# Broadcasting the rows of m by transposes of a repeated column, and denominators in four jobs, in a fused kernel of seven-product matmuls and masked pooling

## The reference, cut to what matters

```
h = gelu(x @ fc1_w.T + fc1_b)                    # 512 -> 2048, exact gelu
x = x + concat(h @ fc2_w.T + fc2_b, h @ experts_w[idx].T + experts_b[idx])   # 384 + 128 columns
attn_in = tanh(x @ W1 + b1)                      # 512 -> 128
scores = attn_in @ v                             # (4, 1024)
mask[j, l] = l <= j | l >= j | l != j            # by the type of the batch
p = softmax(where(mask, scores[l], -1e30), over l)
x = x + (p @ x) / cnt                            # cnt = number of l seen by j
```

## Time and profile before

| | |
|---|---|
| median of the timed runs | 815.1 us |
| profiled execution | 805.86 us |
| its span | 804.2 us |
| mean granted TensorE clock | 0.991 |
| TensorE busy | 781.1 us, 97% |
| VectorE busy | 398.9 us, 50% |
| ScalarE busy | 379.9 us, 47% |
| GpSimd busy | 115.4 us, 14% |
| moved by DMA | 177.11 MB, 220 GB/s |

### The profile page before, as it was taken

The page is one execution under the profiler, slowest core; times in us unless marked ns, Lnnn a source line. Parts: engine busy times, 40 slices in busy tenths (PEclk is TensorE's granted clock), DMA queues, the critical chain, the costliest instruction groups (busy, mean ns, idle before and its releaser), DMA issues.

```text
span 804.2 us, 12318 instructions
## 1 busy us (share of the span) xinstructions
PE 781.1 (97%) x3550; PEld 637.9 (79%) x3550; DVE 398.9 (50%) x681; ACT 379.9 (47%) x641; POOL 115.4 (14%) x157
## 2 busy tenths in 40 slices
PE   6899999999999999999999999999999999999987
PEld 5688887888888888887888888888788888888876
DVE  6855666563453332853535233376245423246665
ACT  6755665443545333552545523445254543344542
POOL 3472230300000130400000022050000002104000
PEclk9999999999999999999999999999999999999998
DMA  7599898777854568866776457886687446697722
GB/s 256 180 365 320 312 348 279 227 229 223 244 173 144 171 197 281 255 208 202 248 215 191 147 162 228 288 246 185 182 277 223 132 150 202 224 282 220 222 67 105
DMA packets 130732, 177.11 MB, mean 220 GB/s; under 512 B 10065, under 2 KB 97633, under 8 KB 130657
## 3 DMA queue, kind: packets, MB, share of 16 engines
q1 hardware_dynamic: 130496, 176.20, 69.5%
q0 software_dynamic: 160, 0.01, 0.1%
HBM read 136.33 MB, written 39.85 MB: 219 GB/s over the span
## 4 chain that ended last, share of the span: by engine, by line
PE 91%; DVE 4%; ACT 2%; issue 1%; DMA 1%; DVEq 0%; SPq 0%; ACTq 0%
PE y L711 14%; PE y L713 14%; PE y L712 14%; PE hA L711 7%; PE hA L713 7%; PE hA L712 7%; PE hF L711 5%; PE hF L713 5%; PE hF L712 5%; PE j L804 2%; DVE xcl L1171 1%; PE j L830 1%; PE j L824 1%; PE j L831 1%; PE j L812 1%
## 5 line engine op out<-in xcount | busy, mean ns | idle before, releaser
L711 PE MATMUL y<-hs,w2c 128*128 128x512 f32 x512 | 202.4, 395 | 3.7 <-DVE w2c L1171 1.4
L713 PE MATMUL y<-hs,w2c 128*128 128x512 f32 x512 | 199.7, 390 | 0.0
L712 PE MATMUL y<-hs,w2c 128*128 128x512 f32 x512 | 199.6, 390 | 0.0
L711 PEld LDWEIGHTS y<-hs,w2c 128*128 128x128 f32 x512 | 96.3, 188 | 26.8 <-DVE hs L1171 4.9
L713 PEld LDWEIGHTS y<-hs,w2c 128*128 128x128 f32 x512 | 96.2, 188 | 20.6
L712 PEld LDWEIGHTS y<-hs,w2c 128*128 128x128 f32 x512 | 96.3, 188 | 19.3
L711 PE MATMUL hA<-xch,w1c 128*128 128x512 f32 x252 | 100.1, 397 | 9.7 <-DVE w1c L1171 5.9
L713 PE MATMUL hA<-xch,w1c 128*128 128x512 f32 x252 | 98.6, 391 | 0.0
L712 PE MATMUL hA<-xcl,w1c 128*128 128x512 f32 x252 | 98.6, 391 | 0.0
L701 POOL TENSOR_TENSOR x1T<-x1T,xnl 128x512 f32<-128x512 f32 x24 | 30.8, 1287 | 439.9 <-DVE x1T L1293 439.9
L966 ACT ACTIVATE hst<-hst,bcol 128x512 f32<-128x512 f32 x62 | 43.8, 721 | 86.4 <-DVE hst L1347 86.4
(11 more groups left out here) (258 smaller groups left out, 1103.5 us busy)
## 6 DMA issues: line engine op xcount, KB each, us to landing
w2c<-w2s SPq DMA_DIRECT2D x114, 384.0 KB, 3.5
w1c<-w1s SPq DMA_DIRECT2D x24, 768.0 KB, 4.5
w2c<-exs SPq DMA_DIRECT2D x114, 128.0 KB, 3.8
w1c<-w1s SPq DMA_DIRECT2D x48, 256.0 KB, 3.4
w1c<-w1s SPq DMA_DIRECT2D x24, 512.0 KB, 4.5
x1T<-in_x SPq DMA_DIRECT2D x32, 256.0 KB, 5.3
w1s<-w1c SPq DMA_DIRECT2D x8, 768.0 KB, 4.2
w2s<-w2c SPq DMA_DIRECT2D x16, 384.0 KB, 5.0
```

Of the source, the lines that this page charges most:

```text
L711: nc.tensor.matmul(ps, ah, bh, start=first, stop=False, skip_group_check=onto)
L712: nc.tensor.matmul(ps, ah, bl, start=False, stop=False, skip_group_check=onto)
L713: return nc.tensor.matmul(ps, al, bh, start=False, stop=last, skip_group_check=onto)
```

## The change

In the loop and the tail a new job `mT` turns m8 once: one fp32 matmul with m8 as the stationary side and an 8x8 identity makes [128, 8], which VectorE copies into a new tile mT. `bc` then is a transpose of a column of mT repeated 128 times, per chunk, in place of an fp32 matmul; it waits for VectorE's copy in place of m8. In the loop `den` is four jobs of two chunks, each of which waits only for the half of Pl and Ws that it reads; in the tail it stays two of four. The slots of mT, bc, den and pool in steps 2 to 6 are others. Jobs that need a bank become 4 more in a pass.

```diff
-BANK = {"xn", "attn", "score", "stats", "bc", "sums", "sums1", "den", "pool"}
+BANK = {"xn", "attn", "score", "stats", "mT", "bc", "sums", "sums1", "den", "pool"}
-          (2, 2): [("bc", 0)], (3, 0): [("bc", 1), ("expE",), ("expPW", 0)], (3, 1): [("sums",), ("sums1",)],
-          (4, 0): [("expPW", 1)], (4, 1): [("den", 0, CH), ("pool", 0)], (4, 2): [("pool", 1)],
-          (5, 0): [("pool", 2), ("pool", 3)], (5, 1): [("pool", 4)], (5, 2): [("pool", 5)], (6, 0): [("pool", 6)],
-          (6, 1): [("pool", 7)]}
+          (2, 2): [("mT",)], (3, 0): [("bc", 0), ("bc", 1), ("expE",), ("expPW", 0)], (3, 1): [("sums",), ("sums1",)],
+          (4, 0): [("expPW", 1), ("den", 0, 2)], (4, 1): [("pool", 0)], (4, 2): [("pool", 1), ("den", 2, 4)],
+          (5, 0): [("pool", 2)], (5, 1): [("pool", 3), ("den", 4, 6)], (5, 2): [("pool", 4)], (6, 0): [("pool", 5), ("den", 6, CH)],
+          (6, 1): [("pool", 6), ("pool", 7)]}
+DENS, DENS_TAIL = [(0, 2), (2, 4), (4, 6), (6, CH)], [(0, BC), (BC, CH)]
...
 TAIL_ORDER: ("stats",), ("expE",), +("mT",), ("bc", 0), ("bc", 1), ...
 TAIL_DVE:   ("stats",), +("mT",), ("expE",), ("xn", 3), ("bc", 0), ("bc", 1), ...
-FULL_BEFORE = {("bc", 1): 1, ("sums",): 2, ("sums1",): 3, ("pool", 0): 4}
+FULL_BEFORE = {("bc", 0): 1, ("bc", 1): 2, ("sums",): 3, ("den", 0, BC): 4}
...
+                elif task[0] == "mT":
+                    pe.wait_ge(chain, b * NCHAIN)
+                    last = nc.tensor.matmul(bank[:, 0:CH], m8[:, :], ident[0:CH, 0:CH], start=True, stop=True)
                 elif task[0] == "bc":
-                    pe.wait_ge(chain, b * NCHAIN)
+                    wait_used(pe, kind, b, at(kind, place, ("mT",)))
                     for i in range(CT):
                         c = task[1] * CT + i
-                        last = nc.tensor.matmul(bank[:, i * P:(i + 1) * P], ident[0:CH, c:c + 1].to_broadcast([CH, P]),
-                                                m8[:, :], start=True, stop=True)
+                        last = nc.tensor.transpose(bank[:, i * P:(i + 1) * P], mT[:, c:c + 1].to_broadcast([P, P]), ident[:, :])
...
-                    pe.wait_ge(Plo, b * 2 + (c1 // BC - 2))
-                    pe.wait_ge(Wlo, b * 2 + (c1 // BC - 2))
+                    pe.wait_ge(Plo, b * 2 + ((c1 - 1) // BC - 1))
+                    pe.wait_ge(Wlo, b * 2 + ((c1 - 1) // BC - 1))
...
+                elif task[0] == "mT":
+                    nc.vector.tensor_copy(mT[:, :], bank[:, 0:CH]).then_inc(used, 1)
...
-                    if c == 0 or kind == "tail" and c == BC:
-                        dve.wait_ge(rd_done, b + c // BC)
+                    dens = DENS_TAIL if kind == "tail" else DENS
+                    firsts = [first for first, _ in dens]
+                    if c in firsts:
+                        dve.wait_ge(rd_done, b * len(DENS) + (firsts.index(c) + 1 - len(DENS)))
```

More of the change, by code:

```diff
@@ L92 @@
 TAIL_ORDER = [("ysum", oc) for oc in range(OC)] + [("x1", oc) for oc in range(OC)] + [
-    ("xn", 0), ("xn", 1), ("attn",), ("xn", 2), ("xn", 3), ("score",), ("stats",), ("expE",), ("bc", 0), ("bc", 1),
+    ("xn", 0), ("xn", 1), ("attn",), ("xn", 2), ("xn", 3), ("score",), ("stats",), ("expE",), ("mT",), ("bc", 0), ("bc", 1),
     ("expPW", 0), ("expPW", 1), ("sums",), ("sums1",), ("den", 0, BC)] + [("pool", c) for c in range(BC)] + [
@@ L100 @@
 TAIL_DVE = [("ysum", 0), ("ysum", 1), ("x1", 0), ("ysum", 2), ("x1", 1), ("ysum", 3), ("x1", 2), ("x1", 3), ("xn", 0),
-            ("xn", 1), ("score",), ("xn", 2), ("stats",), ("expE",), ("xn", 3), ("bc", 0), ("bc", 1),
+            ("xn", 1), ("score",), ("xn", 2), ("stats",), ("mT",), ("expE",), ("xn", 3), ("bc", 0), ("bc", 1),
             ("expPW", 0), ("sums",), ("sums1",), ("expPW", 1), ("den", 0, BC)] + [("pool", c) for c in range(BC)] + [
             ("den", BC, CH)] + [("pool", c) for c in range(BC, CH)]
-FULL_BEFORE = {("bc", 1): 1, ("sums",): 2, ("sums1",): 3, ("pool", 0): 4}
+FULL_BEFORE = {("bc", 0): 1, ("bc", 1): 2, ("sums",): 3, ("den", 0, BC): 4}
 def body(kind):
@@ L235, in build @@
         mc = sb("mc", [CH, 1])
-        m8 = sb("m8", [CH, P])
+        m8, mT = sb("m8", [CH, P]), sb("mT", [P, CH])
         Ef = sb("Ef", [P, CH])
@@ L1176, in task_part @@
                 bank, used = jb[bk], bank_read[bk]
-                if task[0] in ("score", "stats", "bc", "den", "pool"):
+                if task[0] in ("score", "stats", "mT", "bc", "den", "pool"):
                     dve.wait_ge(job_done, job_of(kind, b, pos) + 1)
```

## The result

| | before | after |
|---|---|---|
| timed runs, median | 814.8 us (811.6 to 815.8, 4 runs) | 799.0 us (797.6 to 800.8, 4 runs) |
| profiled execution | 805.86 us | 799.31 us |
| its span | 804.2 us | 797.6 us |
| mean granted clock | 0.991 | 0.994 |

The ratio is 0.985, with a 95% interval of 0.981 to 0.990. The profiled executions differ by 6.6 us only, close to the forecast. So the sum over the profile was good, and what it was applied to was not: the timed executions of before do something that its profiled one did once.

What follows compares the result with a forecast made beforehand. TensorE, busy 97% of the span, was taken to bound the kernel. Three passes -5.0, clock -1.7 and tail -0.7 give -7.4 us, off the 815.1 us median: 807.7 us, range 804.0 to 812.5.

Steps and rivals of the forecast that it cites:

- (a): Broadcast jobs in the loop become transposes: the pair costs 0.89 us instead of 2.58, saving 1.69 us a pass.
- a denominator job: Loop denominators split in four: each job of two chunks 0.76 us, adding 0.24 us a pass in all.
- the stall: TensorE's wait before the loop's denominators for VectorE's second half of Ws goes, saving 0.70 us a pass (bounds 0 and 0.70).
- rival B: VectorE takes the stall over in slots (3,0) and (4,0), giving back 0.6 us a pass: 811.2 us, chance 0.15.
- Sum of a pass: Loop pass: -1.69 transposes, +0.48 mT, +0.24 denominators, -0.70 stall, together -1.67 us; three passes -5.0.
- (g): Tail: sums starts 1.27 us earlier; if the clock's return at 786.96 stands, 0.7 us is saved.
- (f): Clock: the half-speed stretch behind the third pass's denominators disappears, -1.7 us (bounds 0 and -5.1).
- F: Every loop pass of a timed execution now has a half-speed stretch, which the change removes: 804.3 us, chance 0.07.
- C: Tail: the clock comes back later because transposes stand where matmuls stood, price 1.7 us: 809.4 us, chance 0.12.
- D: Loop: the clock falls more often at five places a pass with little column work; 817.9 us, chance 0.06.
- E: Transposes of a repeated column cost what the fp32 broadcast jobs do: 814.0 us, chance 0.05.

## Why the prediction was wrong

**Direction and parts.** (a) was right to 0.01 us, mT was 0.52 for 0.48, a denominator job 0.68 for 0.76, the stall went, and of rival B 0.11 us came true (the wait for add 1), none of it at sums. Sum of a pass -1.67 forecast, -1.67 and -1.63 measured. That the sum meets so well is in part luck: the denominators came out 0.3 us cheaper than counted, and P2 dearer by 0.11 and by 0.08 more behind it. The tail gave 1.0 for 0.7: sums came 1.11 us earlier behind m8 for 1.27, and the clock came back 0.87 us nearer to m8, where (g) had let the moment stand; by half of 0.87 us, an estimate, some 0.4 of the 1.0 is the clock's. Together -5.7 forecast without the clock, -5.0 found in the runs.

**The step that failed is (f), the clock, and with it the step to the median.** The half-speed term was taken as 1.7 us, from the one stretch of the profiled execution, and bounded at 5.1 by three of its length. It measured 8.2 us over all runs, and 10.8 in the pair of samples behind the result (15.8 less 5.0). Two things were wrong in it. A fall can last 6.83 us and not 3.41, so each pass can lose 3.4 us and the bound should have been 10.2: the execution of 815.84 us lost just that at its denominators. And the profiled execution was near the best case: of 69 timed runs one was as short. I had the sign of it before me: the median lay 9.2 us above the profiled execution, and I carried these 9.2 us over to the changed kernel unexplained, though F said that they might be the stretches. Some 3 of the 9.2 are the luck of the three runs behind the 815.1, since the median of all is 812.1. For the changed kernel the median lies at the profiled execution (799.31 profiled, 799.02 median). Had F been worked out with the gap as its measure, 9.2 us lost to the clock beyond the one stretch seen, it would have given 815.1 - 5.7 - 1.7 - 9.2 = 798.5; as it stood, F too was too small, and 804.3 above all runs of the result.

**The rivals.** C did not come: the clock comes back earlier behind m8, not later, in the tail's stretch of 6.82 us as in that of 3.41, and four times as many transposes in the loop leave the clock alone. D did not: with short pieces of little column work the two profiled executions of the changed kernel have no fall in the loop. B came true by 0.11 to 0.19 us a pass of the 0.6. E was refuted by the 0.88 us for the pair.

**Open.** How much of the 8.2 us the fp32 jobs had is not settled. Putting them back costs 3 to 4 us of clock when the two stand in one slot, some 2 when apart, while all three profiled executions of the kernel before have their loop's falls at the denominators only. The fall at 138 us is in batch 0, which the change does not touch. It appears in the profiled executions with the fp32 jobs apart and from 128 partitions and in the two further ones of before, and not in the others. The traces tell them apart by the idle time of TensorE at about 136 us, most of it with no releaser in the profile: 1.82 to 2.02 us in the four with the fall, 0.5 to 1.7 us in nine of the ten without it, 1.89 in the tenth (the denominators in a row). The one other fall ahead of the loop, at 25.2 us in the kernel with two denominator jobs, stands behind a wait of 2.00 us. So these falls seem to go with the length of a wait and not with the edit; no run lengthened or filled it. Why the tail's stretch is 3.41, 6.82 or once 10.2 us long in the profiled executions is not explained.

TensorE where the steps of batch 0 end, in the execution of 815.84 us:

```profile
137.25 0.47 PE L711 MATMUL y<-hs,w2c 128*128 128x512 f32 x1 [2.02 <-DVE hs L1171]
```

## What to carry to other kernels

When the median of the timed runs lies more than their spread above the profiled execution, compare the mean clock of the runs before anything else: here (1 - clock) x span explained the spread of 11 us to a standard deviation of 0.7 us. A row of 24 two-column matmuls between full products, with a wait in front, cost about 2.4 us a pass in clock on top of its own 2.7 us; in pieces of 0.7 or 1.35 us among full-width products no such cost was seen in six to ten runs. A wait of TensorE in a tail can be filled with matmuls that nobody reads (0.9 to 1.9 us in the traces, medians 2.2 us apart).

## What the runs showed that I had not expected

- A fall of the granted clock in the loop lasted 3.41 or 6.83 us. With 8 of the 24 two-column matmuls still to come it was the longer one (267.55 to 274.38, and so in all three passes); with one or none to come it was 3.41 (657.26 to 660.67, and the six others).
- Falls repeat from pass to pass in one execution (266.64, 461.20, 655.76 with the denominators in a row; 267.55, 465.52, 663.50 in the execution of 815.84 us of before), and the executions of one kernel spread over 806 to 817 us.
- 32 transposes of 128 columns at a spacing of 0.11 us kept the clock in six of six runs (0.994 to 0.997); 24 matmuls of two columns at the same spacing, with a wait in front, had 0.987 or less in eight of eight.
- Fp32 matmuls from 8 partitions cost 1.97 us for a pair of jobs, the same from 128 partitions 1.71. The medians are 807.2 and 802.0 us, in samples taken at different times.
